# A four-layer decoder stack on one core: layer 2's first causal row maxima taken in half fills, with the second batch element's queries, keys and values made in between

## The chip, the cores and the metric

The kernel runs on one core of one Trainium2 chip. The metric is the device time of one execution in microseconds (us). Engines are called TensorE (PE in the profile, its weight loads PEld), VectorE (DVE), ScalarE (ACT) and GpSimd (POOL). PSUM has eight banks of 512 fp32 columns.

## The reference

Four transformer layers run one after the other on `x` of 2 batch elements x 512 tokens x 128 features. Only layer 2's causal self attention is touched, with the normalisation ahead of it (16 heads of 8 features):

```python
y = layer_norm(y + h, g3, be3)                # the end of layer 1
h = _ln(x, ln1_g, ln1_b)                      # layer 2
q = (h @ sa_wq + sa_bq).reshape(Bx, Lx, H, HD) * scale
k = (h @ sa_wk + sa_bk).reshape(Bx, Lx, H, HD)
v = (h @ sa_wv + sa_bv).reshape(Bx, Lx, H, HD)
q = _apply_rope(q, cos[:Lx], sin[:Lx])
k = _apply_rope(k, cos[:Lx], sin[:Lx])
a = _attn(q, k, v, causal=True).reshape(Bx, Lx, E)   # softmax needs each row's maximum
```

## The kernel before

Every engine has one instruction stream written out by hand; semaphores (`S(name)`) join them. A *half* is one batch element: 512 tokens in four tiles of 128 (`QB = 4`, `B = 2`). `x` holds tokens in partitions; `qT`, `kT` hold features in partitions.

**Making layer 2's queries and keys.** For each half in turn VectorE adds layer 1's last output to `x` (L1613), takes moments (`moments`, L1568 and L1571), normalises (`normal`, L1577) and multiplies by the gain (L1582); GpSimd adds the shift (`post_norm`, L479); then VectorE takes moments and normalises again for layer 2 (L1568 to L1577). GpSimd makes each reciprocal deviation (L473, L475). TensorE turns the half (`turn_half`, L619), ScalarE copies it to `xT` (L1317), TensorE projects queries and keys (L627, two passes per fp32 product, 512 columns each) and values (L635), ScalarE copies those out (L1506, L1326, L1510), and TensorE swaps the rotary pairs (L1217). GpSimd multiplies by cosines (`by_cosines`, L491); VectorE multiplies the swapped part by sines (L2000) and adds (L2002). GpSimd then makes four masked copies of a half's keys, `km` (`masked`, L496). In the VectorE stream both halves' normalisations stand ahead of the first rotation, and both rotations ahead of the first maximum.

**The maxima.** Heads are handled in 8 groups `g = 4*b + v` (batch element b, v of 4), four heads in each, one per band of 32 rows of the array. For a group, `causal_maxima` computes the scores of each block of 128 queries against its 128, 256, 384 or 512 keys in three fills, `FILLS = ((1, 0), (2,), (3,))`: four matmuls (L782), one per band, into four banks, and four full-height bf16 matmuls (L785) that add the causal mask to the diagonal. The eight banks are two sets of four, used in turn. For each block VectorE reduces the four banks to 128x4 negated maxima (L2012, `heads.max`), which frees the set. After the last group TensorE turns the maxima (`head_shifts`, L796), VectorE builds `q_shift` (L1696), and the exponentials begin (L826 scores, L1396).

TensorE waits for both halves' rotations before the first fill; so do ScalarE's masked keys `k1` (L1514), which the exponentials need. GpSimd adds value biases (L504) and the bias of the next addition (L487) after the masked keys.

Of the kernel before, what the change touches and what calls it, by code (L numbers as in the profile page):

```python
# [10 lines left out]
ALU = mybir.AluOpType  # L11
# [3 lines left out]
P = 128  # L15
D = 128
# [71 lines left out]
FILL_AT = {0: 2 * P, 1: 0, 2: 0, 3: 0}  # L88

ROUND_BEHIND, KEYS_BEHIND, VALUES_BEHIND = 3, 7, 8
# [50 lines left out]
def build(nc, ins, out, stop=99):  # L144
    ctx = ExitStack()
    with ctx:
        def sb(name, shape, dt=F32):
# [5 lines left out]

        families = {
            "one": (["L1.sa", "L1.ca"], dict(s=T, exp=T, t=T, pt=T, o=T, m=T, x=T)),
            "heads": (["L2.sa", "L2.ca"], dict(sc=0, max=4 * T, maxT=B * V, qs=B * V, s=8 * T, e=8 * T,
                                               pv=4 * T, o=B * V, ot=B * V, out=B * V)),
            "ints": (["L3.sa"], dict(s=PAIRS, nm=PAIRS, m=PAIRS, exp=2 * PAIRS, recip=PAIRS // 2, rounded=2 * PAIRS,
                                     pt=PAIRS, pv=PAIRS)),
# [260 lines left out]
        def _(pool):  # L420
# [72 lines left out]
            def masked(b):  # L493
                pool.wait_ge(S("L2.sa.rope"), 2 * b + 2)
                for v in range(V):
# [12 lines left out]
            if stop >= 1:  # L508
                for h in range(B):
                    rstds_of("L1.ln1", h)  # L510
                    post_norm("L1.ln1", 1, h)
                for h in range(B):
                    rstds_of("L1.ln2", h)
                    post_norm("L1.ln2", 3, h)
                    add_bias("L1.ff", "L1.ln2.x", h, h + 1)
                for h in range(B):
                    rstds_of("L1.ln3", h)
                    if h and stop >= 2:
                        pool.wait_ge(S("rope.loaded"), 32)
                        by_cosines(0, qT, 0)  # L520
                    post_norm("L1.ln3", 5, h)
                    if h and stop >= 2:
                        by_cosines(1, kT, 0)
                    if stop >= 2:
                        rstds_of("L2.ln1", h)
                if stop >= 2:
                    for side, src in enumerate((qT, kT)):
                        pool.wait_ge(S("L2.sa.rope"), side + 1)
                        by_cosines(side, src, 1)
                    masked(0)  # L530
                    masked(1)
                    value_biases()
                    for h in range(B):
                        add_bias("L2.ca0", "L2.ln1.xh", h, h + 1)
            def diagonals():

                for b in range(B):
# [76 lines left out]
        def _(pe):  # L614
# [143 lines left out]
            def project_half(name, wo, k, bank):  # L758
# [3 lines left out]
                    mm = pe.matmul(o, tile(xT, k * QB + t), wo, start=True, stop=True)  # L762
                mm.then_inc(S(f"{name}.o"), 1)

            def causal_maxima():

                for g in range(B * V):
                    b, v = divmod(g, V)
                    pe.wait_ge(S("L2.sa.keys"), g + 1)
                    for f, blocks in enumerate(FILLS):  # L770
                        bank = 4 * ((3 * g + f) % 2)
                        if f == 0 and g >= 1:
                            pe.wait_ge(S("heads.max"), QB * g - 1)
                        if f == 1 and g >= 1:
                            pe.wait_ge(S("heads.max"), QB * g)
                        if f == 2:
                            pe.wait_ge(S("heads.max"), QB * g + 2)
                        for qb in blocks:
                            c, n = FILL_AT[qb], (qb + 1) * P
                            for j in range(BANDS):  # L780
                                r = slice(BAND * j, BAND * (j + 1))
                                pe.matmul(ps[:, bank + j, c:c + n], qT[r, b * N + qb * P:b * N + (qb + 1) * P],  # L782
                                          km[r, v, b * N:b * N + n], start=True, stop=False)
                            for j in range(BANDS):
                                mm = pe.matmul(ps[:, bank + j, c + n - P:c + n], ident16[:, :], hide_q[:, :],  # L785
                                               start=False, stop=True)
                        mm.then_inc(S("L2.sa.fill"), 1)

            def head_shifts(name, quads, groups, bank):

# [418 lines left out]


            if stop >= 2:
                for k in range(B):
                    turn_half(xh, "L2.ln1.xh", k)
                    qkv("L2.sa", W["L2_xattn_sa_wq"], W["L2_xattn_sa_wk"], W["L2_xattn_sa_wv"], k)
                    for side, src in enumerate((qT, kT)):
                        pe.wait_ge(S("L2.sa.qk"), 2 * k + side + 1)
                        pe.matmul(ps[:, 2 * side + k, :], swap[:, :], half(src, k), start=True, stop=True  # L1217
                                  ).then_inc(S("L2.sa.swapped"), 1)
                pe.wait_ge(S("L2.sa.vraw"), B)
                pe.wait_ge(S("L2.sa.rope"), 2 * B)  # L1220
                causal_maxima()
                head_shifts("L2.sa", 4 * T - 1, range(V), lambda g: g)
                head_shifts("L2.sa", 4 * T, range(V, B * V), lambda g: g)
# [81 lines left out]
        def _(act):  # L1305
# [194 lines left out]
                state_out("L1.ff", col("L1_xattn_g2"), col("L1_xattn_be2"), [1])  # L1500
                hidden("L1.ff", ACT.Relu, "L1_xattn_b_ff1", HIDDEN_1, range(FC, B * FC))
            if stop >= 2:
                for k in range(B):
                    state_out("L2.sa", col("L2_xattn_ln1_g"), col("L2_xattn_ln1_b"), [k])
                    act.wait_ge(S("L2.sa.q.mm"), k + 1)
                    act.activation(half(qT, k), ps[:, 2 + k, :], ACT.Identity, scale=HEAD_SCALE, bias=bq_scaled[:, :]  # L1506
                                   ).then_inc(S("L2.sa.qk"), 1)
                    project_out(kT, "L2.sa.k.mm", 4, "L2.sa.qk", col("L2_xattn_sa_bk"), [k])
                    act.wait_ge(S("L2.sa.v.mm"), k + 1)
                    act.activation(v_one[:, :, k, :, 0:DH], ps[:, 6 + k, :].rearrange("p (t h d) -> p t h d", h=H, d=DH),  # L1510
                                   ACT.Copy).then_inc(S("L2.sa.vraw"), 1)
                act.wait_ge(S("L2.sa.rope"), 2 * B)
                for v in range(V):
# [42 lines left out]
        def _(dve):  # L1556
# [423 lines left out]
            if stop >= 1:  # L1980
                for k in range(B):
                    dve.wait_ge(S("L1.sa.v.mm"), k + 1)
                    dve.tensor_copy(half_rows(v_rows, k), bank_rows(6 + k)).then_inc(S("L1.sa.v"), 1)
                dve.wait_ge(S("spread.loaded"), 16)
                single_head()
                for k in range(B):
                    add_to_x("L1.ff", OUTPUTS_1, [k])
                    moments("L1.ln3", k, "L1.ff.x", 1)
                    normal("L1.ln3", k, to=4)
                    if stop >= 2:  # L1990
                        moments("L2.ln1", k, "L1.ln3.x", 1)
                        normal("L2.ln1", k)


            if stop >= 2:
                for k in range(B):
                    for side, src in enumerate((qT, kT)):
                        a, b = half(ta, side), half(tb, side)
                        dve.wait_ge(S("L2.sa.swapped"), 2 * k + side + 1)
                        then(dve.tensor_tensor(b, ps[:, 2 * side + k, :], sin_t[:, :], ALU.mult))  # L2000
                        dve.wait_ge(S("L2.sa.cos"), 2 * k + side + 1)
                        dve.tensor_tensor(half(src, k), a, b, ALU.add).then_inc(S("L2.sa.rope"), 1)  # L2002
                for g in range(B * V):
                    b, v = divmod(g, V)
                    for f, blocks in enumerate(FILLS):
                        bank = 4 * ((3 * g + f) % 2)
                        dve.wait_ge(S("L2.sa.fill"), len(FILLS) * g + f + 1)
                        for qb in blocks:
                            at = ((b * QB + qb) * V + v) * P
                            nm = neg_max[:, at:at + P].rearrange("p (j c) -> p j c", c=BAND)[:, :, spare_row(v)]  # L2010
                            c = FILL_AT[qb]
                            dve.tensor_reduce(nm, ps[:, bank:bank + 4, c:c + (qb + 1) * P], AX, ALU.max, negate=True  # L2012
                                              ).then_inc(S("heads.max"), 1)
# [172 lines left out]
```

## Time and profile before

| | us |
|---|---|
| median of 3 runs | 543.89 (541.73 to 545.26) |
| the profiled execution | 544.86 |
| its span, first to last instruction | 543.1 |
| busy: TensorE / VectorE | 398.2 / 365.9 |
| busy: ScalarE / GpSimd | 249.8 / 239.3 |

The span is from the first to the last instruction; the profiled execution took 1.8 us more than its span. An engine's busy time is a mean over stages with different limits: the stage of this change lies between 98 and 181 us of the span. What a group of instructions waited for stands in brackets behind it, as [idle before <-releaser].

### The profile page before, as it was taken

Reading aid. Unit: us, or ns where it says so; the run is one execution under the profiler, and the core shown is the slowest. Engines: PE = TensorE matmul, PEld = TensorE weight load, DVE = VectorE, ACT = ScalarE, POOL = GpSimd, SP = SyncE. Lnnn points to the kernel's source line nnn. Section 1 sums busy time; section 2 is a strip of 40 time slices with the busy share of each in tenths; the row PEclk is TensorE's granted clock in tenths of the full one; section 3 lists DMA queues with packets and bytes.
Section 4 is the critical chain, followed back from the end, with each engine's and each line's share of the span. In section 5 each row is a group of like instructions: output and inputs, shape, how many; then the busy total and the mean of one; then the engine's idle time right before and its main releaser. Section 6 shows DMA issues by size and latency. Waiting matters only on the chain.

```text
span 543.1 us, 8012 instructions
## 1 busy us (share of the span) xinstructions
PE 398.2 (73%) x2719; PEld 208.0 (38%) x2719; DVE 365.9 (67%) x810; ACT 249.8 (46%) x489; POOL 239.3 (44%) x377
## 2 busy tenths in 40 slices
PE   6979768847888999998988772566665664532697
PEld 3736644624334533434243550222232222221546
DVE  1654655364999711338584469999989898989542
ACT  2213423323100367660626327899977793334341
POOL 4033114355300244441301315999978895435420
PEclk9759855997899999999999995555555556665599
DMA  9400000000000000000000002798877586113301
GB/s 262 152 1 1 4 0 1 1 0 0 1 2 1 1 1 2 1 1 1 0 1 2 1 2 39 135 151 144 154 120 127 106 142 129 27 31 66 72 1 39
DMA packets 88975, 26.09 MB, mean 48 GB/s; under 512 B 81061, under 2 KB 88167, under 8 KB 88935
## 3 DMA queue, kind: packets, MB, share of 16 engines
q1 hardware_dynamic: 88935, 25.58, 24.1%
q8 instruction: 22, 0.36, 0.3%
q14 instruction: 18, 0.15, 0.1%
HBM read 5.61 MB, written 0.52 MB: 11 GB/s over the span
## 4 chain that ended last, share of the span: by engine, by line
PE 38%; DVE 32%; POOL 19%; issue 6%; ACT 2%; DMA 2%; POOLq 0%; DVEq 0%; ACTq 0%
POOL k_stack L565 13%; DVE k_stack L2012 8%; PE ps L826 5%; PE ps L841 4%; POOL stats L556 3%; PE ps L627 3%; PE ps L728 3%; DVE stats L2092 3%; PE ps L738 2%; DVE xh L1577 2%; DVE cr_max L1815 2%; DVE st L1568 2%; DVE cr_sum L1829 2%; PE ps L619 2%; PE ps L904 2%
## 5 line engine op out<-in xcount | busy, mean ns | idle before, releaser
L2092 DVE TENSOR_REDUCE stats<-ps 128x2 f32<-128x1024 f32 x64 | 77.7, 1213 | 2.4 <-PE ps L1255 2.0
L1533 ACT ACTIVATE e_buf<-ps,stats,sders 128x512 f32<-128x512 f32 x88 | 67.6, 773 | 18.4 <-POOL stats L556 18.4
L1275 PE MATMUL ps<-k_stack,q_stack 128*32 128x128 bf16 x512 | 38.2, 305 | 41.6 <-DVE k_stack L2105 41.4
L565 POOL TENSOR_SCALAR k_stack<-e_buf,stats 128x512 int16<-128x512 f32 x88 | 63.0, 728 | 2.1 <-DVE stats L2099 1.5
L1396 ACT ACTIVATE e_buf<-ps 128x1024 f32<-128x1024 f32 (+3 forms) x44 | 28.2, 710 | 58.5 <-PE ps L826 58.5
L1275 PEld LDWEIGHTS ps<-k_stack,q_stack 128*32 128x32 bf16 x512 | 22.1, 128 | 70.9 <-DVE k_stack L2105 68.8
L422 POOL TENSOR_SCALAR_AFFINE_SELECT e_buf<-e_buf 128x256 f32<-128x256 f32 x44 | 17.8, 413 | 67.2 <-ACT e_buf L1396 66.5
L473 POOL TENSOR_SCALAR rstd<-mv 128x4 f32<-128x4 f32 x18 | 4.1, 230 | 97.4 <-DVE mv L1571 94.4
L1255 PE MATMUL ps<-q_stack 32*128 32x512 bf16 x128 | 37.8, 591 | 12.2 <-ACT e_buf L1533 8.7
L2012 DVE TENSOR_REDUCE k_stack<-ps 128x4 f32<-128x1024 f32 (+3 forms) x32 | 45.0, 1481 | 2.5 <-PE ps L785 2.5
L782 PE MATMUL ps<-q_stack,qk 32*128 32x256 f32 (+3 forms) x256 | 27.6, 501 | 10.3 <-DVE k_stack L2012 7.4
L826 PE MATMUL ps<-k_stack,q_stack 32*128 32x512 f32 (+3 forms) x256 | 34.7, 478 | 0.6 <-ACT e_buf L1396 0.4
L1533 ACT ACTIVATE t_buf<-ps,stats,sders 128x512 f32<-128x512 f32 x40 | 30.8, 774 | 6.4 <-POOL stats L556 6.3
L556 POOL TENSOR_SCALAR stats<-stats,sders 128x2 f32<-128x2 f32 x64 | 23.7, 370 | 17.5 <-DVE stats L2092 17.4
L1703 DVE COPY v_rows<-ps 128x512 f32<-128x512 f32 x16 | 11.0, 689 | 29.8 <-PE ps L841 22.9
L1317 ACT ACTIVATE xT<-ps,cols 128x512 f32<-128x512 f32 x16 | 12.4, 776 | 38.5 <-PE ps L619 38.5
L1613 DVE TENSOR_TENSOR x<-ps,x 128x512 f32<-128x512 f32 x14 | 9.7, 690 | 30.3 <-PE ps L728 16.2
L627 PE MATMUL ps<-xT,wsq 128*128 128x512 f32 x36 | 25.7, 834 | 4.7 <-ACT xT L1317 4.7
L1577 DVE TENSOR_SCALAR xh<-x,mv,rstd 128x128 f32<-128x128 f32 x68 | 20.3, 361 | 12.8 <-POOL rstd L475 12.8
L565 POOL TENSOR_SCALAR k_stack<-t_buf,stats 128x512 int16<-128x512 f32 x40 | 28.3, 719 | 0.6 <-DVE stats L2099 0.2
L619 PE MATMUL ps<-ident,xh 128*128 128x128 f32 x80 | 15.6, 327 | 17.6 <-DVE xh L1577 16.5
L2105 DVE TENSOR_SCALAR k_stack<-k_stack 128x1024 bf16<-128x1024 int16 x64 | 27.9, 441 | 0.2
(269 smaller groups left out, 880.8 us busy)
## 6 DMA issues: line engine op xcount, KB each, us to landing
wsq<-in_squares SPq DMA_DIRECT2D x3, 384.0 KB, 5.0
k_stack<-k_stack SPq DMA_TRANSPOSE x64, 3.1
spread<-in_spread SPq DMA_DIRECT2D x1, 896.0 KB, 6.7
x<-in_x SPq DMA_DIRECT2D x1, 512.0 KB, 4.5
l_w<-in_L_xattn_W_ff SPq DMA_DIRECT2D x2, 256.0 KB, 7.1
l_w<-in_L_xattn_fc_w SPq DMA_DIRECT2D x2, 256.0 KB, 7.8
l_w<-in_L_xattn_ff_w SPq DMA_DIRECT2D x1, 512.0 KB, 8.8
out<-x SPq DMA_DIRECT2D x2, 256.0 KB, 2.3
```

Of the source, the lines that this page charges most:

```text
L556: pool.tensor_scalar(stats[:, 1, c:c + 2], stats[:, 0, c:c + 2], sders[:, 8:9], None, ALU.mult).then_inc(S("ints.m"), 1)
L565: pool.tensor_scalar(t_rows[n % TURNING][:, j, :], e_ring[n % len(e_ring)][:, j, :], stats[:, 2, c:c + 1], 0.0, ALU.mult, ALU.add).then_in ...
L627: return pe.matmul(ps[:, bank, :], w, half(xT, k), start=True, stop=True)
L826: mm = pe.matmul(ps[:, 2 * slot + j % 2, 0:N - kb * P], k1[r, v, b * N + kb * P:b * N + (kb + 1) * P], q_shift[r, b, v, kb * P:N], start=T ...
L1255: mm = pe.matmul(ps[:, 2 * (n % 3) + j % 2, :], tile(q_int, b * QB + qb)[r, :], k_band[r, v, b * N:(b + 1) * N], start=True, stop=True)
L1275: mm = pe.matmul(ps[BAND * band:BAND * (band + 1), 7, qb * P:(qb + 1) * P], v_band[:, kb, b, V * band + v, :], t_keys[n % len(t_keys)][:, ...
L1396: act.activation(e_ring[n % len(e_ring)][:, :, 0:N - kb * P], ps[:, 2 * (n % 3):2 * (n % 3) + 2, 0:N - kb * P], ACT.Exp).then_inc(S("heads ...
L1533: act.activation(e_ring[n % len(e_ring)][:, j, :], ps[:, 2 * (n % 3) + j, :], ACT.Exp, bias=stats[:, 1, c:c + 1], scale=sders[:, 8:9], acc ...
L1577: ins = dve.tensor_scalar(xh[:, t, :], x[:, t, :], mv[:, t, 0:1], rstd[:, t:t + 1], ALU.subtract, ALU.mult)
L2012: dve.tensor_reduce(nm, ps[:, bank:bank + 4, c:c + (qb + 1) * P], AX, ALU.max, negate=True).then_inc(S("heads.max"), 1)
L2092: dve.tensor_reduce(stats[:, 0, c:c + 2], ps[:, 2 * (n % 3):2 * (n % 3) + 2, :], AX, ALU.max, negate=True).then_inc(S("ints.nm"), 1)
L2105: dve.tensor_scalar(t_keys[n % len(t_keys)], t_turned[n % TURNING], QMAX, None, ALU.min).then_inc(S("ints.pt"), 1)
```

## The change

1. The first two of the eight groups (`HALVED = 2`) are taken in *half fills*: each fill of a group is made twice, for bands 0 and 1 and for bands 2 and 3, into two banks each. There are 12 half fills (`HALF_FILLS`), and they go round three pairs of banks, 0 to 5. A half fill may start once the third one before it has been reduced (`L2.sa.half`). VectorE's reductions of these are 128x2 out of two banks.
2. Banks 6 and 7 serve the second half meanwhile: TensorE turns it after half fill 2 (counted from 0), projects queries after 3 and keys after 5, swaps after 7 and 8, projects values after 9. VectorE normalises the second half after half fill 1 and rotates its queries after 7 and its keys after 9.
3. The other six groups are filled and reduced as before, through two sets of four banks.
4. VectorE applies gain and shift of layer 1's last normalisation itself (`scaled_and_shifted`), for both halves; GpSimd's `post_norm` of it is gone. The second half's gain, shift and layer 2 moments stand behind the first half's rotations in the VectorE stream.
5. GpSimd masks the first half's keys for groups 0 and 1, makes the second half's deviation, masks for groups 2 and 3, and then goes on to the second half's cosines and keys.

```diff
+HALVED = 2
+HALF_FILLS = [(g, blocks, pair) for g in range(HALVED) for blocks in FILLS for pair in range(2)]
+TURN_BEHIND, QUERIES_BEHIND, KEYS_MADE_BEHIND, SWAP_Q_BEHIND, SWAP_K_BEHIND, VALUES_MADE_BEHIND = 2, 3, 5, 7, 8, 9
+SECOND_NORMAL_BEHIND, ROPE_Q_BEHIND, ROPE_K_BEHIND = 1, 7, 9
...
+                by_cosines(0, qT, 0)
+                by_cosines(1, kT, 0)
+                masked(0, (0, 1))
+                rstds_of("L2.ln1", 1)
+                masked(0, (2, 3))
+                for side, src in enumerate((qT, kT)):
+                    pool.wait_ge(S("L2.sa.rope"), side + 1)
+                    by_cosines(side, src, 1)
+                masked(1)
+                value_biases()
...
+            def fill(g, blocks, bank, bands):
+                b, v = divmod(g, V)
+                for qb in blocks:
+                    c, n = FILL_AT[qb], (qb + 1) * P
+                    for i, j in enumerate(bands):
+                        r = slice(BAND * j, BAND * (j + 1))
+                        pe.matmul(ps[:, bank + i, c:c + n], qT[r, b * N + qb * P:b * N + (qb + 1) * P],
+                                  km[r, v, b * N:b * N + n], start=True, stop=False)
+                    for i, j in enumerate(bands):
+                        mm = pe.matmul(ps[:, bank + i, c + n - P:c + n], ident16[:, :], hide_q[:, :],
+                                       start=False, stop=True)
+                mm.then_inc(S("L2.sa.fill"), 1)
...
+                for n, (g, blocks, pair) in enumerate(HALF_FILLS):
+                    pe.wait_ge(S("L2.sa.keys"), g + 1)
+                    if n >= 3:
+                        pe.wait_ge(S("L2.sa.half"), n - 2)
+                    fill(g, blocks, 2 * (n % 3), (2 * pair, 2 * pair + 1))
+                    if n == TURN_BEHIND:
+                        turn_half(xh, "L2.ln1.xh", 1, bank=7)
+                    if n == QUERIES_BEHIND:
+                        pe.wait_ge(S("state.T"), state("L2.sa", 1))
+                        pe.wait_ge(S("L2.sa.vraw"), 1)
+                        project("L2.sa", W["L2_xattn_sa_wq"], 1, 6).then_inc(S("L2.sa.q.mm"), 1)
+                    if n == KEYS_MADE_BEHIND:
+                        project("L2.sa", W["L2_xattn_sa_wk"], 1, 7).then_inc(S("L2.sa.k.mm"), 1)
+                    if n == SWAP_Q_BEHIND:
+                        swapped(1, 0, 6)
+                    if n == SWAP_K_BEHIND:
+                        swapped(1, 1, 7)
+                    if n == VALUES_MADE_BEHIND:
+                        pe.wait_ge(S("L2.sa.rope"), 3)
+                        for t in range(QB):
+                            mm = pe.matmul(ps[:, 6, t * P:(t + 1) * P], tile(xT, QB + t), W["L2_xattn_sa_wv"],
+                                           start=True, stop=True)
...
+                def scaled_and_shifted(name, k, g):
+                    scale, shift = (spread[:, i, :].unsqueeze(1).broadcast_to([P, QB, D]) for i in (g, g + 1))
+                    dve.wait_ge(S(f"{name}.xh"), count(name, "xh") + k + 1)
+                    then(dve.tensor_tensor(half_rows(x, k), half_rows(xh, k), scale, ALU.mult))
+                    dve.tensor_tensor(half_rows(x, k), half_rows(x, k), shift, ALU.add).then_inc(S(f"{name}.x"), 1)
...
+                for side in range(2):
+                    rope(0, side, 2 * side)
+                scaled_and_shifted("L1.ln3", 1, 4)
+                moments("L2.ln1", 1, "L1.ln3.x", 1)
+                for n, (g, blocks, pair) in enumerate(HALF_FILLS):
+                    dve.wait_ge(S("L2.sa.fill"), n + 1)
+                    for ins in filled(g, blocks, 2 * (n % 3), slice(2 * pair, 2 * pair + 2)):
+                        last = ins
+                    last.then_inc(S("L2.sa.half"), 1)
+                    if n == SECOND_NORMAL_BEHIND:
+                        normal("L2.ln1", 1)
+                    if n == ROPE_Q_BEHIND:
+                        rope(1, 0, 6)
+                    if n == ROPE_K_BEHIND:
+                        rope(1, 1, 7)
```

## Rows read from the trace of the kernel before

**Rows 1.** Busy time by stretch: ahead of the maxima, and the maxima.
```profile
core 0: us, PE busy (x) PEld busy (x) DVE busy (x) ACT busy (x) POOL busy (x), PEclk, DMA share, GB/s
135.40:181.10 45.70, 37.86 (x378) 18.59 (x376) 45.03 (x33) 2.84 (x3) 5.74 (x6) 0.96 0.00 1
98.00:135.50 37.50, 24.89 (x130) 15.29 (x128) 19.20 (x60) 10.92 (x15) 17.58 (x21) 0.91 0.00 0
```

**Rows 2.** The chain that ended last, in order of time: start, us, what.
```profile
105.35 1.27 POOL x L479
...
133.67 0.71 PE ps L782 x8
...
139.65 41.43 DVE k_stack L2012 x29
```

**Rows 3.** VectorE's maxima by shape: count, busy us, mean ns, idle before.
```profile
L2012 DVE TENSOR_REDUCE k_stack<-ps 128x4 f32<-128x2048 f32 x8 | 18.2, 2281 | 0.2 <-PE ps L785 0.2
L2012 DVE TENSOR_REDUCE k_stack<-ps 128x4 f32<-128x1536 f32 x8 | 14.0, 1748 | 0.3 <-PE ps L785 0.3
L2012 DVE TENSOR_REDUCE k_stack<-ps 128x4 f32<-128x1024 f32 x8 | 9.7, 1215 | 1.9 <-PE ps L785 1.9
L2012 DVE TENSOR_REDUCE k_stack<-ps 128x4 f32<-128x512 f32 x8 | 5.4, 680 | 0.0
```

**Rows 4.** VectorE in order of time ahead of the maxima: start, us, instructions.
```profile
109.41 1.12 DVE L1577 TENSOR_SCALAR xh<-x,mv,rstd 128x128 f32<-128x128 f32 x4 [1.48 <-POOL rstd L475]
...
113.91 2.07 DVE L1577 TENSOR_SCALAR xh<-x,mv,rstd 128x128 f32<-128x128 f32 x4 [1.46 <-POOL rstd L475]
...
121.88 0.68 DVE L2000 TENSOR_TENSOR tb<-ps,sin_t 128x512 f32<-128x512 f32 x1
...
135.52 1.83 DVE L2012 TENSOR_REDUCE k_stack<-ps 128x4 f32<-128x1024 f32 x2 [1.95 <-PE ps L785]
```

**Rows 5.** GpSimd in order of time in the same stretch.
```profile
114.10 1.29 POOL L491 TENSOR_TENSOR ta<-qk,cos_t 128x512 f32<-128x512 f32 x1 [0.23 <-ACT qk L1506]
...
119.77 1.04 POOL L475 TENSOR_TENSOR rstd<-rstd,minus_half 128x4 f32<-128x4 f32 x1
...
129.90 3.14 POOL L496 TENSOR_SCALAR q_stack<-qk,band_mask 128x512 f32<-128x512 f32 x4
```

**Rows 6.** TensorE in order of time: parts of one group's fills, at steady pace.
```profile
151.07 0.71 PE L782 MATMUL ps<-q_stack,qk 32*128 32x256 f32 x8 [0.29 <-DVE k_stack L2012]
...
151.72 0.40 PE L785 MATMUL ps<-hide_q,ident 128*128 128x128 bf16 x4
...
152.05 0.50 PE L782 MATMUL ps<-q_stack,qk 32*128 32x128 f32 x8
...
152.48 0.40 PE L785 MATMUL ps<-hide_q,ident 128*128 128x128 bf16 x4
...
154.91 1.14 PE L782 MATMUL ps<-q_stack,qk 32*128 32x512 f32 x8 [0.47 <-DVE k_stack L2012]
...
155.98 0.40 PE L785 MATMUL ps<-hide_q,ident 128*128 128x128 bf16 x4
```

**Rows 7.** TensorE later, in layer 2's cross attention: two bands alone.
```profile
260.08 1.08 PE L904 MATMUL ps<-k_stack,k 32*77 32x512 f32 x4 [0.66 <-DVE k_stack L1696]
```

**Rows 8.** TensorE in order of time around the first half's swaps.
```profile
113.93 1.05 PE L635 MATMUL ps<-wsq,xT 128*128 128x128 f32 x8
114.82 1.88 PE L1217 MATMUL ps<-qk,swap 128*128 128x512 f32 x4
122.02 1.11 PE L619 MATMUL ps<-ident,xh 128*128 128x128 f32 x4 [5.32 <-DVE xh L1577]
```

**Rows 9.** Busy time by short stretch, with TensorE's granted clock (PEclk).
```profile
118.30:121.70 3.40, 0.00 (x0) 0.00 (x0) 1.89 (x12) 0.00 (x0) 2.24 (x3) 1.00 0.00 0
121.70:125.10 3.40, 2.21 (x6) 1.30 (x7) 2.85 (x6) 0.78 (x1) 0.00 (x0) 0.51 0.00 0
...
131.90:135.40 3.50, 1.73 (x24) 1.11 (x24) 1.64 (x2) 1.79 (x2) 2.87 (x5) 1.00 0.00 0
135.40:138.80 3.40, 3.40 (x22) 1.37 (x20) 2.98 (x3) 2.84 (x3) 3.40 (x5) 0.50 0.02 5
```

More of the change, by code:

```diff
@@ L515, in _ @@
                     add_bias("L1.ff", "L1.ln2.x", h, h + 1)
-                for h in range(B):
[L517 to L534, printed above, removed]
+                rstds_of("L1.ln3", 0)
+                rstds_of("L2.ln1", 0)
+                rstds_of("L1.ln3", 1)
+                pool.wait_ge(S("rope.loaded"), 32)
+                by_cosines(0, qT, 0)
[8 more added lines that the diff above has]
+                value_biases()
+                for h in range(B):
+                    add_bias("L2.ca0", "L2.ln1.xh", h, h + 1)
             def diagonals():
@@ L765, in causal_maxima @@
             def causal_maxima():
-                for g in range(B * V):
-                    b, v = divmod(g, V)
+                for g in range(HALVED, B * V):
+                    done = QB * (g - HALVED)
                     pe.wait_ge(S("L2.sa.keys"), g + 1)
                     for f, blocks in enumerate(FILLS):
[L771 to L775, printed above, removed]
-                        if f == 2:
[L777 to L787, printed above, removed]
@@ L789, in head_shifts @@
+                        if f == 2:
+                            pe.wait_ge(S("heads.max"), done + 2)
+                        fill(g, blocks, bank, range(BANDS))
             def head_shifts(name, quads, groups, bank):
@@ L1985, in _ @@
                 single_head()
[L1986 to L1992, printed above, removed]
-            if stop >= 2:
[L1996 to L2003, printed above, removed]
-                    b, v = divmod(g, V)
-                    for f, blocks in enumerate(FILLS):
[L2006 to L2013, printed above, removed]
@@ new lines, in _, with rope, filled @@
+                moments("L1.ln3", 0, "L1.ff.x", 1)
+                normal("L1.ln3", 0)
+                scaled_and_shifted("L1.ln3", 0, 4)
+                moments("L2.ln1", 0, "L1.ln3.x", 1)
+                normal("L2.ln1", 0)
+                add_to_x("L1.ff", OUTPUTS_1, [1])
+                moments("L1.ln3", 1, "L1.ff.x", 1)
+                normal("L1.ln3", 1)
+            if stop >= 2:
+                def rope(k, side, bank):
+                    a, b, dst = half(ta, side), half(tb, side), half((qT, kT)[side], k)
+                    dve.wait_ge(S("L2.sa.swapped"), 2 * k + side + 1)
+                    then(dve.tensor_tensor(b, ps[:, bank, :], sin_t[:, :], ALU.mult))
+                    dve.wait_ge(S("L2.sa.cos"), 2 * k + side + 1)
+                    dve.tensor_tensor(dst, a, b, ALU.add).then_inc(S("L2.sa.rope"), 1)
+                def filled(g, blocks, bank, bands):
+                    b, v = divmod(g, V)
+                    for qb in blocks:
+                        at = ((b * QB + qb) * V + v) * P
+                        nm = neg_max[:, at:at + P].rearrange("p (j c) -> p j c", c=BAND)[:, bands, spare_row(v)]
+                        c, n = FILL_AT[qb], bands.stop - bands.start
+                        ins = dve.tensor_reduce(nm, ps[:, bank:bank + n, c:c + (qb + 1) * P], AX, ALU.max, negate=True)
+                        yield ins
+                for side in range(2):
+                    rope(0, side, 2 * side)
[12 more added lines that the diff above has]
+                        rope(1, 1, 7)
+                for g in range(HALVED, B * V):
+                    for f, blocks in enumerate(FILLS):
+                        m = 3 * (g - HALVED) + f
+                        dve.wait_ge(S("L2.sa.fill"), len(HALF_FILLS) + m + 1)
+                        for ins in filled(g, blocks, 4 * (m % 2), slice(0, BANDS)):
+                            ins.then_inc(S("heads.max"), 1)
```

54 lines of the change are left out of this document (35 added, 19 removed).

## The prediction

> **What bounds the kernel now.** I read the busy time by stretch first. From 135.4 to 181.1 us VectorE is busy 45.0 of 45.7 us, while TensorE is busy 37.9 [rows 1]: the maxima are VectorE's. From 98 to 135.5 VectorE is busy only 19.2 of 37.5 us [rows 1]. The chain of work then shows how these two join: one chain leads through additions, norms, projections and rotations to the first fill at 133.67, and from 139.65 it is 29 reductions without a break, 41.43 us, to 181.08 [rows 2]. The first reduction starts at 135.52 [rows 4]. So the stage ends when VectorE has done 45 us of maxima after a start that waits for both batch elements, although the first element's keys are ready some ten microseconds sooner. What the change can give is read at 181.08, the end of the last reduction: everything behind it (turned maxima, exponentials, the later layers) starts from there and keeps its order.
>
> **The change, part by part.** I follow the new order and carry one clock, the time in the span.
>
> *The shift on VectorE.* GpSimd's shift takes 1.27 us [rows 2]; on VectorE it is a 128x512 operation like the sine product, 0.68 [rows 4]. With the hop it saves 0.62 for the first half, and everything up to the second half's layer 1 norm moves forward by 0.62: that norm starts at 113.91 - 0.62 = 113.29. It still meets the first cosine product on GpSimd, so it keeps its 2.07 us and ends at 115.36.
>
> *The first rotation earlier.* The second half's gain, shift, moments and layer 2 norm no longer stand ahead of the rotation. Its inputs are there: the swaps start at 114.82 - 0.62 = 114.20 [rows 8], the two cosines end by 116.1 (two of 1.29 [rows 5] from 113.5). Four operations of 0.68 with their hops, 2.75 us, end at 118.13. Two masked copies follow on GpSimd; one costs 0.65 to 0.8 (3.14 for four [rows 5]).
>
> *A collision.* VectorE's gain and shift now run beside GpSimd's masked copies. The row shows that such work blocks: the same four normalising operations took 2.07 us where a GpSimd product started 0.19 us into them, and 1.12 where none did [rows 4, 5]. I price it at 0.6 (about one masked copy) here, and again at 0.6 where the second layer 2 norm meets the masks for groups 2 and 3; the bounds for each are 0, if the two miss each other, and 1.3, two masked copies. The reductions I leave alone: beside GpSimd's copies the first two took 1.83 [rows 4], their unhindered length by [rows 3].
>
> By the Trainium skill (SBUF — State Buffer, Who interferes with whom), whichever starts first holds the shared ports for its whole instruction when VectorE has two SBUF inputs or a two-port mode. By that rule gain and shift could each meet a copy, 1.3 instead of 0.6, and the last reduction would come 0.7 later; the trace's 2.07 against 1.12 is a blocking of about one instruction.
>
> So the first half fill starts at 119.6, and VectorE ends gain, shift (2.0 with the collision) and moments (1.3) at 121.5.
>
> *Half fills on TensorE.* A fill of 256 columns takes 0.65 from its start to its masks, of 128 0.43, of 512 1.07; 384 lies between, 0.86 [rows 6]. The four masks occupy 0.33 [rows 6], two of them 0.22. Does a matmul group on two bands cost half of one on four? The trace has two bands alone: 512 columns, 1.08 us [rows 7], beside 1.14 for four [rows 6]. So it costs the same, and a group's maxima cost TensorE nearly twice. Half fills occupy 0.65 + 0.22 + 0.43 + 0.22 = 1.52, 0.86 + 0.22 = 1.08 and 1.07 + 0.22 = 1.29; four of each are 15.5 us, where two whole groups took 1.74 + 1.19 + 1.40 = 4.3 each, 8.7 together.
>
> *The second half's work on TensorE.* Turning 0.44 (four passes of 0.11), two projections and two swaps of 0.86 each (1.88 for two swaps with the tail of the last [rows 8]), values 0.87 (eight passes within 1.05 [rows 8]): 4.7 us. With the half fills that is 20.3 us from 119.6. By the new order there is one wait in it: behind half fill 2 (done at 123.7) TensorE needs the second half's norm. The moments are there at 121.5, GpSimd's deviation (0.23 and 1.04 [rows 5]) at 122.9; VectorE reduces half fills 0 and 1 first, then norms for 1.1 + 0.6 and ends at 125.3. TensorE loses 1.7 us there, and the half fills 3 to 11 stand behind that turn. ScalarE's copies lie under half fill 3 and later ones.
>
> *Half reductions on VectorE.* From [rows 3], 512 elements more cost 0.533 us, so 1.04 ns each and 0.146 fixed; back to back, 29 of them fit in 41.43 us, 0.08 less each than their durations. So a half reduction of 256, 512, 768, 1024 elements takes 0.33, 0.60, 0.86, 1.13: 11.7 us for the twelve half fills against 11.2 for two whole groups, 0.5 us for eight more instructions. The 256 is below every row, by the line through the others; were it as dear as the 512, it would add 0.27 four times.
>
> *Who sets the pace there.* VectorE has 11.7 + 1.7 + 2 x 1.4 = 16.2 us from 121.5; TensorE has 20.3 + 1.7 from 119.6. TensorE sets it: half fill 11 starts at 140.3 and is reduced by 142.8. The first whole fill needs the bank pairs of half fills 9 and 10; it starts near 141.8, takes 1.8, and VectorE waits 0.8 us and starts on it at 143.6. Six groups follow at 5.6 us each (5.92 by [rows 3] less four overlaps of 0.08): the last reduction ends at 177.4. The second half's keys, masks, values and ScalarE's four `k1` copies lie under these 34 us.
>
> *The clock.* TensorE was granted full speed until 121.7 and half of it (1.2 GHz) after a gap of 5.3 us without a matmul [rows 8, 9]; it fell again at 135.4 after a stretch in which it was busy 1.73 of 3.5 us [rows 9]. Over the maxima it was at 0.96 on average [rows 1], so that fall was short. In the new order TensorE idles from about 116.1 to 119.6, 3.5 us, between those two cases. I take one fall, 121.7 to 125.1, at a cost of 0.95: the half fills in it take double, part of it under the wait for the norm. The bounds are none (0) and a fall from 118.3 to 128.6 (3.1).
>
> **Sum.** 177.4 + 0.95 = 178.4 against 181.08: 2.7 us sooner. The profiled execution took 544.86, so 542.2; the median of the runs is 0.97 below that execution, so 541.2.
>
> **The rivals.**
>
> *Nothing is won.* The clock is at half from 118.3 to 128.6, or both collisions cost 1.3 (1.4 more) and the 256-element reductions 1.1: the last reduction ends near 180.7, and the time is 543.5. For it: two falls in this very stretch [rows 9]. Against: the new gap is shorter than the one that cost two steps. Chance 0.18.
>
> *More is won.* Full speed throughout gives 177.4, or 540.2, and cheap collisions up to 1.5 more, 538.7. Chance 0.14.
>
> *VectorE-bound after all.* If the second pair's matmuls overlapped the masks of the first, so that a half fill cost about half a fill, VectorE would run through: 121.5 + 16.2 + 0.8 + 33.7 = 172.2, 8.9 us sooner, 535.0. What speaks against it is that a mask is 128 rows high and starts only when the bands have finished [rows 6]. The Trainium skill, TensorEngine Tiling (Array Packing), Key Properties, says that a change of tiling mode drains the array. By that rule this way is closed, and the trace agrees: 1.07 us from a 512-column start to its masks. Chance 0.11.
>
> *Slower.* TensorE, at two bands and waiting for VectorE, is held at half speed through all half fills (118.3 to 143): they and the second half's work take twice as long, the last reduction ends at 187.8, and the time is 550.6. It costs more than it gives from the point where the half clock lasts beyond 129.5. For it: a stretch busy for half its time lost the clock [rows 9]. Against: from 119.6 on TensorE is nearly always busy, and in the maxima it kept 0.96 of full speed on average with 37.9 busy of 45.7 us [rows 1]. Chance 0.09.
>
> **How the numbers follow.** My forecast has the remaining 0.48. A change of 1% is 5.4 us, about what a measurement of this kernel can tell from none. Faster by over 1% is the VectorE-bound way and a thread of the second rival, 0.12; slower by over 1% 0.09; within 1% 0.79. The forecast's own range is 539.5 to 543. The range for the time leaves out the VectorE-bound way and the slower one: 537.8 at the cheap end of the collisions, 546.3 for a clock at half until about 134.
>
> **What would show it.** In the profile after: GpSimd's L479 work at 105 and 117 gone; first half fill at 119.6 and first half reduction at 121.5 (was 135.52); half fills of 1.3 us for 512 columns; TensorE waiting 1 to 2 us for the norm behind half fill 2; VectorE idle some 5 us in all between 121.5 and 143.6; whole groups at 5.6 us as before; last reduction near 178. The prediction is wrong if a half fill costs much less than 1.3 us, if the granted clock stays at half beyond 128, or if the time after the last reduction (363.8 us to the end of this execution) is not the same.

## The result

| | us |
|---|---|
| median after (4 runs) | 557.16 (554.87 to 557.68) |
| median before, measured with it (4 runs) | 543.88 (541.73 to 545.26) |
| ratio after / before | 1.027, 95% interval 1.023 to 1.032 |
| profiled execution after | 554.87, its span 553.1 |

The change made the kernel 2.7% slower. The stage itself can be compared from one event to another: from the first half's last layer 1 norm (L1577 before, L1621 after) to the end of the last maximum. Before it runs from 103.43 to 181.08, 77.6 us. After it runs from 99.18 to 190.80, 91.6 us: 14.0 us more, where the prediction had 2.7 less. What follows is the same to half a microsecond (362.0 us of span before, 362.3 after). So the profiled spans differ by 10.0 us only: the stage began 4.25 us sooner in this one execution, because the clock had come back sooner in the code ahead of it, which the change does not touch (in all thirteen traces of this document the norm starts about 9 to 10.5 us after that return, wherever it falls). The busy time of the same window (us, the engines, granted clock, DMA share, GB/s), of the kernel before:

```profile
89.80:94.40 4.60, 4.60 (x7) 1.92 (x6) 2.79 (x13) 1.57 (x3) 1.45 (x3) 0.50 0.00 0
```

and of the kernel after, where the clock was already back at full:

```profile
89.80:94.40 4.60, 3.73 (x26) 2.77 (x25) 0.43 (x1) 1.37 (x2) 2.53 (x2) 1.00 0.01 4
```

The busy time by stretch of the kernel after, to be read beside [rows 1, 9]: the pause, the start of the first half fill, the rest of the half fills, the whole fills up to the clock's return, and the rest.

```profile
core 0: us, PE busy (x) PEld busy (x) DVE busy (x) ACT busy (x) POOL busy (x), PEclk, DMA share, GB/s
112.00:116.00 4.00, 0.00 (x0) 0.00 (x0) 3.90 (x7) 0.00 (x0) 1.17 (x2) 1.00 0.00 0
116.00:117.20 1.20, 1.17 (x10) 0.74 (x10) 1.17 (x5) 0.00 (x0) 0.98 (x1) 0.98 0.00 0
117.20:152.70 35.50, 35.27 (x111) 13.54 (x108) 15.72 (x28) 6.72 (x8) 9.15 (x12) 0.50 0.00 1
152.70:161.50 8.80, 8.80 (x57) 3.95 (x56) 5.82 (x5) 0.57 (x1) 3.46 (x3) 0.50 0.01 2
161.50:190.80 29.30, 24.04 (x252) 12.30 (x248) 29.30 (x22) 0.00 (x0) 0.00 (x0) 1.00 0.00 1
```

TensorE was busy for 35.27 of 35.5 us and was granted half its clock (1.2 GHz) all the while. It got the other half back at 161.5, 8.8 us after the whole fills had begun. VectorE had work for 15.7 of those 35.5 us, so it was not what TensorE waited for.

VectorE in order of time answers to [rows 4]. The bracket behind a reduction is the time it stood idle for a fill:

```profile
109.03 3.04 DVE L1621 TENSOR_SCALAR xh<-x,mv,rstd 128x128 f32<-128x128 f32 x4 [1.48 <-POOL rstd L481]
...
117.83 1.02 DVE L2062 TENSOR_REDUCE k_stack<-ps 128x2 f32<-128x512 f32 x2
...
129.67 1.23 DVE L2062 TENSOR_REDUCE k_stack<-ps 128x2 f32<-128x1024 f32 x1 [3.19 <-PE ps L778]
...
136.35 1.02 DVE L2062 TENSOR_REDUCE k_stack<-ps 128x2 f32<-128x512 f32 x2 [3.12 <-PE ps L778]
...
160.48 30.31 DVE L2062 TENSOR_REDUCE k_stack<-ps 128x4 f32<-128x2048 f32 x21 [0.80 <-PE ps L778]
```

The first reduction stands 18.65 us after the norm (before: 32.09), so the early start was had. TensorE in order of time, answering to [rows 6]: the start of the first half fill at full clock, the second half's turning, and two half fills at half clock.

```profile
116.03 0.70 PE L775 MATMUL ps<-q_stack,qk 32*128 32x256 f32 x4 [4.21 <-POOL q_stack L502]
...
122.46 1.11 PE L623 MATMUL ps<-ident,xh 128*128 128x128 f32 x4 [0.23 <-DVE xh L1621]
...
127.23 2.08 PE L775 MATMUL ps<-q_stack,qk 32*128 32x512 f32 x4
129.24 0.39 PE L778 MATMUL ps<-hide_q,ident 128*128 128x128 bf16 x2
129.56 2.08 PE L775 MATMUL ps<-q_stack,qk 32*128 32x512 f32 x4
```

A half fill of 512 columns is 2.33 us from start to start, against 1.29 forecast at full clock. The chain of work runs through TensorE alone from 122.5 to 160.5.

### The profile page after: what moved, and what is told of

Its sections match the earlier page's. It is cut to its first block, busy times and chain, and to the rows that moved or that the text cites. A ratio compares the mean times of both kernels' runs of the same rounds, so it can differ in the third digit from the quotient of the medians.

```text
span 553.1 us, 8030 instructions
## 1 busy us (share of the span) xinstructions
PE 413.1 (75%) x2719; PEld 210.4 (38%) x2719; DVE 369.6 (67%) x820; ACT 249.5 (45%) x489; POOL 237.0 (43%) x375
## 4 chain that ended last, share of the span: by engine, by line
PE 42%; DVE 29%; POOL 18%; issue 6%; ACT 2%; DMA 2%; POOLq 0%; DVEq 0%; ACTq 0%
POOL k_stack L569 13%; DVE k_stack L2062 6%; PE ps L873 5%; PE ps L775 5%; PE ps L888 4%; POOL stats L560 3%; PE ps L631 3%; PE ps L732 3%; DVE stats L2164 3%; PE ps L742 2%; DVE xh L1621 2%; DVE cr_max L1859 2%; PE ps L623 2%; DVE cr_sum L1873 2%; PE ps L766 2%
## 5 line engine op out<-in xcount | busy, mean ns | idle before, releaser
L2164 DVE TENSOR_REDUCE stats<-ps 128x2 f32<-128x1024 f32 x64 | 77.6, 1213 | 2.4 <-PE ps L1299 2.0
L1577 ACT ACTIVATE e_buf<-ps,stats,sders 128x512 f32<-128x512 f32 x88 | 67.6, 774 | 19.1 <-POOL stats L560 19.1
L1319 PE MATMUL ps<-k_stack,q_stack 128*32 128x128 bf16 x512 | 37.9, 305 | 42.6 <-DVE k_stack L2177 42.6
L2062 DVE TENSOR_REDUCE k_stack<-ps 128x4 f32<-128x1024 f32 (+7 forms) x40 | 46.7, 1219 | 21.9 <-PE ps L778 21.8
L775 PE MATMUL ps<-q_stack,qk 32*128 32x256 f32 (+3 forms) x256 | 45.0, 608 | 9.1 <-DVE k_stack L2062 4.8
L1577 ACT ACTIVATE t_buf<-ps,stats,sders 128x512 f32<-128x512 f32 x40 | 30.8, 773 | 6.4 <-POOL stats L560 6.3
L1621 DVE TENSOR_SCALAR xh<-x,mv,rstd 128x128 f32<-128x128 f32 x68 | 21.2, 375 | 11.5 <-POOL rstd L481 11.5
```

What stands on the lines that cost most here:

```text
L775: pe.matmul(ps[:, bank + i, c:c + n], qT[r, b * N + qb * P:b * N + (qb + 1) * P], km[r, v, b * N:b * N + n], start=True, stop=False)
L1319: mm = pe.matmul(ps[BAND * band:BAND * (band + 1), 7, qb * P:(qb + 1) * P], v_band[:, kb, b, V * band + v, :], t_keys[n % len(t_keys)][:, ...
L1577: act.activation(e_ring[n % len(e_ring)][:, j, :], ps[:, 2 * (n % 3) + j, :], ACT.Exp, bias=stats[:, 1, c:c + 1], scale=sders[:, 8:9], acc ...
L1621: ins = dve.tensor_scalar(xh[:, t, :], x[:, t, :], mv[:, t, 0:1], rstd[:, t:t + 1], ALU.subtract, ALU.mult)
L2062: ins = dve.tensor_reduce(nm, ps[:, bank:bank + n, c:c + (qb + 1) * P], AX, ALU.max, negate=True)
L2164: dve.tensor_reduce(stats[:, 0, c:c + 2], ps[:, 2 * (n % 3):2 * (n % 3) + 2, :], AX, ALU.max, negate=True).then_inc(S("ints.nm"), 1)
```

## The experiments

Two theories stood against each other. **W (width)**: matmuls on two of the four bands leave TensorE at half clock however busy it is. **G (gap)**: the clock was lost to the 4.2 us pause ahead of the half fills, and would have held without it.

**The pause filled** (`gap_filled`).

```diff
                 pe.wait_ge(S("L2.sa.vraw"), 1)
+                for _ in range(4):
+                    pe.matmul(ps[:, 1, :], ident[:, :], half(xT, 0), start=True, stop=True)
                 first_maxima_of_self()
```

> The changed kernel with four extra full-height matmuls of 512 columns (results unused, into a free bank) in TensorE's pause between the first half's swaps and the first half fill. Theory W (width): TensorE loses its full clock because the half fills run on two of four bands; the clock falls within them all the same, and the time stays at 555 to 557 us. Theory G (gap): the pause of 4 us takes the clock away; with it filled the clock stays at full speed through the half fills, the stage goes as predicted, and the time is near 540 us.

Measured: 555.94 us, ratio to before 1.024 (1.018 to 1.030), within W's 555 to 557. TensorE in order of time:

```profile
110.34 3.77 PE L1265 MATMUL ps<-xT,ident 128*128 128x512 f32 x8
114.48 0.71 PE L775 MATMUL ps<-q_stack,qk 32*128 32x256 f32 x4 [0.38 <-POOL q_stack L502]
115.13 0.28 PE L778 MATMUL ps<-hide_q,ident 128*128 128x128 bf16 x2
115.34 0.49 PE L775 MATMUL ps<-q_stack,qk 32*128 32x128 f32 x4
115.76 0.28 PE L778 MATMUL ps<-hide_q,ident 128*128 128x128 bf16 x2
115.98 0.71 PE L775 MATMUL ps<-q_stack,qk 32*128 32x256 f32 x4
```

and the busy time and the clock by stretch (this execution's records list full speed as 0.95):

```profile
110.00:114.80 4.80, 4.42 (x12) 1.74 (x12) 4.70 (x8) 0.00 (x0) 1.70 (x3) 0.95 0.00 0
114.80:117.80 3.00, 3.00 (x26) 1.65 (x24) 2.54 (x12) 0.00 (x0) 2.07 (x4) 0.95 0.00 0
117.80:150.00 32.20, 31.23 (x92) 11.62 (x88) 14.26 (x21) 6.50 (x8) 7.59 (x9) 0.50 0.00 1
```

With 0.4 us of pause left and TensorE busy all of 114.8 to 117.8, the clock fell at 117.8 all the same, two half fills in, and stayed down until 155.3. So G does not account for the loss: without the pause the time is that of the changed kernel. That a pause can take the clock as well is not excluded by this; `both_pairs` below bears on it.

**Half fills alone** (`halves_alone`): the kernel before, with groups 0 and 1 in half fills (`first_maxima_of_self`, banks 0 to 5) and nothing between them; `causal_maxima` keeps groups 2 to 7.

```diff
+                first_maxima_of_self()
                 causal_maxima()
```

> halves_waiting without the extra waits: the half fills of groups 0 and 1 alone, in the order of the kernel before. Theory W: the clock stays at half through them; 2 us less than halves_waiting for the waits, 557 to 558 us, some 3 per cent slower than before; the changed kernel minus this is then what the new order alone gives back (about -1 to -3 us).

Measured: 558.17 us against 542.08, ratio 1.027 (1.021 to 1.032), 0.2 above the range expected. The half fills run from 129.3 to 155.3; the stretch at half clock, which ends 6.2 us behind them:

```profile
130.80:161.50 30.70, 30.70 (x129) 11.93 (x128) 15.61 (x19) 3.06 (x3) 5.93 (x6) 0.50 0.00 1
```

In the old order the half fills alone cost the whole loss. The stage took 93.6 us; in the changed kernel, with the new order, it took 91.6, so the new order gave 2.0 us back.

**The same with the idle bands at work** (`halves_waiting` against `halves_four_bands`). Both wait for the end of the half fill before (the extra matmuls of successive half fills share banks 6 and 7). The second, to which the last four added lines belong, also runs each block on the other two bands, results unused:

```diff
                 for n, (g, blocks, pair) in enumerate(HALF_FILLS):
...
+                    if n >= 1:
+                        pe.wait_ge(S("L2.sa.fill"), n)
...
+                    for i, j in enumerate(j for j in range(BANDS) if j not in bands):
+                        r = slice(BAND * j, BAND * (j + 1))
+                        pe.matmul(ps[:, 6 + i, c:c + n], qT[r, b * N + qb * P:b * N + (qb + 1) * P],
+                                  km[r, v, b * N:b * N + n], start=True, stop=True)
```

> The kernel before, in its old order, with groups 0 and 1 taken in half fills and nothing put between them; each half fill also waits for the end of the one before it (so that it compares with halves_four_bands). W: the clock stays at half from about 135 us until some 9 us after the last half fill; two groups take 27 us on TensorE where VectorE needs 11.7, and the time is 560 to 564 us. If width does not matter, the clock comes back after one step of 3.4 us as in the kernel before; two groups take 17, and the time is 549 to 551 us.

> halves_waiting with the two idle bands given the same matmuls into banks 6 and 7, results unused: the same order and waits, the same fills, all four bands at work, and by the rows of before no time added at equal clock. W: the clock comes back within one or two steps, and the time is 549 to 552 us. If width does not matter it equals halves_waiting within 1 us, or is slower.

Measured: 559.63 us (ratio 1.032, 1.027 to 1.036) and 551.54 us (1.016, 1.009 to 1.023). The first of these is just below the 560 to 564 expected, the second within its 549 to 552. The stretches of the half fills, of `halves_waiting`:

```profile
132.10:159.80 27.70, 26.20 (x92) 9.65 (x92) 12.32 (x16) 2.85 (x3) 6.15 (x7) 0.50 0.00 1
```

and of `halves_four_bands`, where the clock came back at 140.5, after 6.8 us (the last 1.6 us of the second line are whole fills):

```profile
133.70:140.50 6.80, 6.50 (x40) 2.64 (x40) 2.90 (x5) 2.84 (x3) 5.73 (x6) 0.50 0.01 2
140.50:154.20 13.70, 12.51 (x125) 5.51 (x124) 9.83 (x11) 0.00 (x0) 0.00 (x0) 1.00 0.01 2
```

The share of time in which TensorE is busy is nearly the same in the first line (26.2 of 27.7, 95%) and in the last two (19.0 of 20.5, 93%). Both kernels lost the clock within 2 us of their first half fill, behind a pause of 2.5 to 2.9 us. With two bands it stayed at half from 132.1 to 162.8, 30.7 us, and came back 4.0 us after four bands had started; with four bands it stayed at half for 6.8 us. Twice the work within the same instructions' time made the kernel 8 us faster. So W is shown for what it says of the time at half clock: what kept the clock down is that half of the bands stood empty. Whether the rows count or the number of running matmuls, this pair cannot tell, since both double. The trace of the kernel before speaks for the rows: there full-height matmuls that run one behind the other (L738, from 88.84 on, in the window of that kernel shown with the result) had the full clock back at 94.4, 5.6 us later, so one matmul at a time is enough where it fills them.

**Both pairs issued together** (`both_pairs`): the changed kernel, with the matmuls of a block on all four bands before its masks; banks and reductions still go by pairs.

```diff
+                    for k, qb in enumerate(FILLS[f]):
...
+                        for pair in range(2):
+                            if k == 0 and 2 * w + pair >= 3:
+                                pe.wait_ge(S("L2.sa.half"), 2 * w + pair - 2)
+                            for i in range(2):
+                                j = 2 * pair + i
+                                r = slice(BAND * j, BAND * (j + 1))
+                                pe.matmul(ps[:, banks[pair] + i, c:c + n], qT[r, b * N + qb * P:b * N + (qb + 1) * P],
+                                          km[r, v, b * N:b * N + n], start=True, stop=False)
+                        for pair in range(2):
+                            for i in range(2):
+                                mm = pe.matmul(ps[:, banks[pair] + i, c + n - P:c + n], ident16[:, :], hide_q[:, :],
+                                               start=False, stop=True)
```

> The changed kernel with the matmuls of both pairs of bands issued together (four bands at work at once), through the same three pairs of banks, each pair still reduced by itself; TensorE turns the second half after whole fill 1, projects queries and keys after 2, swaps after 3 and 4, values after 4. W: the clock, lost in the pause, comes back within one or two steps; a group costs TensorE 4.3 us instead of 7.8, VectorE waits some 3 us in all; the last reduction is 5 to 7 us sooner than in the kernel before relative to layer 1's last norm, and the time is 537 to 540 us. G: the pause still takes the clock, and it stays away as long as in the changed kernel, some 44 us: 552 us or more.

Measured: 540.45 us, ratio 0.997 (0.993 to 1.000). The changed kernel's ratio is 1.027, so it is 3% faster than that one, and G's 552 us or more is out. Against the kernel before it is 1.3 us, which can hardly be told from none, and just outside the 537 to 540 expected. The stage took 75.8 us, 1.9 less than before, where 5 to 7 less were expected: the clock was at half from 118.7 to 129.0, across the first fills, longer than forecast, and again from 139.2 to 146.1:

```profile
115.00:129.00 14.00, 11.10 (x55) 5.53 (x56) 11.58 (x25) 0.95 (x2) 4.78 (x6) 0.63 0.01 1
129.00:139.20 10.20, 8.38 (x66) 3.93 (x65) 7.82 (x13) 3.17 (x5) 3.79 (x4) 1.00 0.00 1
139.20:146.10 6.90, 6.90 (x44) 2.90 (x44) 4.46 (x4) 3.27 (x3) 6.17 (x7) 0.51 0.00 0
```

The first fall came 0.8 us into the first fill, behind an unfilled pause of 4.2 us, with all four bands at work. So here a pause did cost the clock, and in the changed kernel it may have taken it first as well. What the half fills added is that it was lost without the pause too (`gap_filled`), and that it did not come back for 44.4 us.

**Its pauses filled** (`both_pairs_gap`, `both_pairs_warm`, `both_pairs_warmer`): full-height matmuls, results unused, put where TensorE waits. The first has four in the pause ahead of the first fill, the second one more ahead of the first fill of group 2, the third one more behind whole fill 1 (in this order in the diff).

```diff
+                for _ in range(4):
+                    pe.matmul(ps[:, 1, :], ident[:, :], half(xT, 0), start=True, stop=True)
                 first_maxima_of_self()
...
+                    if w == 5:
+                        pe.wait_ge(S("L2.sa.rope"), 4)
+                        pe.matmul(ps[:, 7, :], ident[:, :], half(xT, 0), start=True, stop=True)
...
                     if w == 1:
+                        pe.matmul(ps[:, 6, :], ident[:, :], half(xT, 0), start=True, stop=True)
                         turn_half(xh, "L2.ln1.xh", 1, bank=7)
```

> both_pairs with four extra full-height matmuls of 512 columns (results unused) in TensorE's pause between the first half's swaps and the first fill. In both_pairs the clock was at half from 118.7 to 129.0 us, where TensorE was busy nearly all the time, and again from 139.2 to 146.1. If the pause causes the first fall, and four bands at work keep the clock, it is at full speed there; by the fills' rows that is worth 2 to 3 us of both_pairs' time, so 537 to 538.5 us where both_pairs has 540.5. If the first fills lose the clock even so (as in gap_filled), the time is both_pairs' within 1 us.

> both_pairs_gap with one more unused full-height matmul while TensorE waits for the last paired reductions, ahead of the first fill in the old manner, where the clock fell the second time. If that wait of 1.7 us causes the second fall, it goes too, worth another 1 to 1.5 us: 536 to 537.5 us. Otherwise the time is that of both_pairs_gap.

> both_pairs_warm once more, with more rounds: 1.3 per cent faster than the kernel before, 0.9 to 1.7.

> both_pairs_warm with one more unused matmul while TensorE waits 1.2 us for the second half's norm behind whole fill 1, where the clock of both_pairs_gap fell at 122.7 us and that of both_pairs_warm did not. If that wait is what takes the clock in some of the executions, the slow ones among them go: the median is 1 to 2 us below both_pairs_warm. If not, the two are equal within 1 us.

| | median us | before beside it | ratio (95%) | stage, us |
|---|---|---|---|---|
| `both_pairs_gap` | 538.86 | 542.08 | 0.990 (0.982 to 0.998) | 75.7 |
| `both_pairs_warm` | 536.24 | 542.08 | 0.987 (0.980 to 0.994) | 70.9 |
| `both_pairs_warm_again` | 536.93 | 542.24 | 0.992 (0.988 to 0.995) | 70.9 |
| `both_pairs_warmer` | 535.82 | 542.24 | 0.988 (0.982 to 0.995) | 70.9 |

Filling the first pause alone did not keep the clock in the profiled execution (half from 122.7 to 129.6 and from 139.8 to 146.6), and its time against `both_pairs` on another set of runs settles nothing. With the wait ahead of group 2 filled too, the clock stayed full through the stage in the three profiled executions. The fall at 122.7 is not explained by that filling, which comes later: `both_pairs_warm` has the same code and the same wait of 1.18 us there, and kept its clock. The turning behind that wait, of `both_pairs_gap` and then of `both_pairs_warm`:

```profile
123.41 1.11 PE L623 MATMUL ps<-ident,xh 128*128 128x128 f32 x4 [1.18 <-DVE xh L1637]
...
119.80 0.66 PE L623 MATMUL ps<-ident,xh 128*128 128x128 f32 x4 [1.18 <-DVE xh L1640]
```

So what a wait of this length does to the clock differs from one execution to another, and how often each kernel keeps it is not known from three traces. The repetition came to 0.8% where 0.9 to 1.7 was expected. The added matmul of `both_pairs_warmer` cannot be told from none. The best is 6.4 us faster than the kernel before; its stretch, up to group 2 and from there:

```profile
109.00:134.00 25.00, 23.28 (x141) 11.10 (x139) 22.99 (x41) 4.79 (x8) 10.42 (x12) 1.00 0.00 1
134.00:170.00 36.00, 29.57 (x306) 14.84 (x304) 35.14 (x27) 3.95 (x4) 6.82 (x8) 1.00 0.01 1
```

**How much of that is the clock** (`before_warm`): the kernel before with its own two pauses filled.

```diff
                 for k in range(B):
+                    for _ in range(5 * k):
+                        pe.matmul(ps[:, 1, :], ident[:, :], half(xT, 0), start=True, stop=True)
                     turn_half(xh, "L2.ln1.xh", k)
...
                 pe.wait_ge(S("L2.sa.vraw"), B)
+                for _ in range(3):
+                    pe.matmul(ps[:, 7, :], ident[:, :], half(xT, 0), start=True, stop=True)
                 pe.wait_ge(S("L2.sa.rope"), 2 * B)
```

> The kernel before with unused full-height matmuls in two pauses of TensorE: five between the first half's swaps and the second half's turning, three between the second half's swaps and the first fill. It tells how much of both_pairs_warm's gain is the clock and how much the order. In the kernel before the clock was at half for 6.8 and 3.4 us there; by the rows of that stretch (projections 3.78 us at half against 1.98, turning 1.11 against 0.66, first fills 0.5 to 1 us late) the clock is worth 2.5 to 3 us: 539 to 540 us where the kernel before has 542. If it is 536 or less, the order in both_pairs_warm gives nothing.

Measured: 539.00 us, ratio 0.994 (0.991 to 0.997), the stage 73.9 us, at full clock throughout. So of the stage's 6.8 us (77.65 to 70.87) the clock is 3.8, and the order with four bands at work, the shift on VectorE included, 3.0. This split is read from profiled executions, one of `before_warm` and three of the others, which took 70.9 each; the intervals of the whole times, 0.991 to 0.997 here and 0.988 to 0.995 for `both_pairs_warm_again`, overlap. The interleaving is worth something in the stage; the half fills were not.

**The shift alone** (`shift_alone`).

```diff
-                    normal("L1.ln3", k, to=4)
+                    normal("L1.ln3", k)
+                    scaled_and_shifted("L1.ln3", k, 4)
...
-                    post_norm("L1.ln3", 5, h)
```

> The kernel before with only one part of the change: VectorE applies the gain and the shift of layer 1's last norm, for both halves; GpSimd's shift is gone; the order is the old one. By the prediction's step it saves 0.6 us for each half on the chain, 1.2 in all: 0.1 to 0.4 per cent faster than the kernel before. If GpSimd's cosine product then blocks VectorE's two-input operations, it saves nothing.

Measured: 542.63 us against 542.08, ratio 0.998 (0.995 to 1.002): nothing that can be told. The stage took 77.3 us, 0.3 less where 1.2 was forecast. With the shift gone from GpSimd, both cosine products follow one another there, and VectorE's norm meets the two, which costs 1.0 us more than meeting one:

```profile
111.12 3.04 DVE L1576 TENSOR_SCALAR xh<-x,mv,rstd 128x128 f32<-128x128 f32 x4 [1.47 <-POOL rstd L475]
...
111.30 2.52 POOL L491 TENSOR_TENSOR ta<-qk,cos_t 128x512 f32<-128x512 f32 x2 [0.22 <-ACT qk L1505]
```

## Why the prediction was wrong

*The step that failed* is the one on the clock. It asked only how long TensorE would pause, took one fall of 3.4 us at 0.95 us (the fall of the kernel before at 121.7 had itself lasted until 128.5), and let the half fills count as full activity because TensorE would be busy nearly all the time. The clock was at half for 44.4 us, 117.15 to 161.53. At 116.0, after the pause, the first half fill still ran at full speed (0.70 for 256 columns), and `gap_filled` showed that the clock is lost without the pause too. The argument against the slower rival, full clock through the maxima with 37.9 of 45.7 us busy [rows 1], came from fills on four bands and was carried over to two. The two-band matmuls at full clock of [rows 7] were 1.08 us between full-height work, a turning at 258.77 and a projection at 261.10.

The Trainium skill (TensorE: Matmul & The Clock Gate, Part 1, What's actually happening) says that the gate is set by how busy the PE has been recently. The rows differ if busy means the share of time: 35.27 of 35.5 us at 0.50 here. The measurement decides: how much of the array is filled counts too.

*The rival that came true* is the slower one, chance 0.09, and only in part. Two bands at work and half speed through all half fills is what happened; that TensorE would be "waiting for VectorE" is not, for it was busy 35.27 of 35.5 us. Its size was too small, 550.6 against 557.2, mostly by its own sum: it says that the half fills and the second half's work take twice as long, but it adds 10.4 us, about half of the stretch from 118.3 to 143 as it would be at full clock. From the first half fill to the first whole one the forecast had 22.2 us (119.6 to 141.8), and the trace has 36.7 (116.03 to 152.69), 14.5 more. Besides, the clock came back 8.8 us after the last half fill, not with it, and three whole fills ran at half speed too.

*The terms, from norm to last reduction* (forecast 75.0 us with its clock term, measured 91.6):

- The start. The first half fill came 16.85 us after the norm, forecast 16.2: 0.7 late. The collision of the second layer 1 norm with both cosine products (3.04 instead of 2.07) costs 1.0; the rotation and the first masked copy came 0.3 closer behind it than forecast. The two collisions with the masks, priced at 0.6 each, are not on this path: the first cost 0.37 (the shift, 1.06 instead of 0.69), the second nothing (the layer 2 norm took 1.11).
- The twelve half fills and the second half's work, from the first half fill to the first reduction of group 2: 39.8 us (116.03 to 155.79), forecast 24.95 (119.6 to 143.6, and 0.95 for the clock): 14.8 more. At full clock the term looks right: `gap_filled` shows 0.65 + 0.21 + 0.42 + 0.22 = 1.50 for the first half fill, forecast 1.52. Two bands do cost what four cost: 0.65 from the start of the 256 columns to their masks in both cases.
- Within that term, the wait for the second half's norm behind half fill 2, forecast 1.7, was 0.23, since TensorE itself came late.
- The six whole groups: 35.0 us (155.79 to 190.80), forecast 33.8: 1.2 more, at the half clock.
- The half reductions were right: 0.69 for 512 elements and 0.42 for 256, both within 0.02 of the line through [rows 3].

0.7 + 14.8 + 1.2 is the whole difference of 16.7. The 14.8 and the 1.2 are the clock's: the step that could be compared at full clock fits (1.50 against 1.52), and at half clock a half fill of 512 columns is 1.8 times its forecast. That everything behind the stage would keep its time was right.

## What to carry to other kernels

A band left empty is not only lost throughput: on this chip it kept TensorE at half clock while it was busy without a pause. When a PSUM shortage suggests fills in halves, split the buffers and the reductions but issue the matmuls so that all bands run together, as `both_pairs` does. That alone does not hold the clock: there it fell behind a pause with four bands at work too. An empty pause of TensorE ahead of a stage that it sets can be worth filling with unused full-height matmuls: that alone gave the old kernel 0.6%.

## What the runs showed of the hardware

- The clock was lost with TensorE busy 3.0 of 3.0 us on half fills (`gap_filled`, 114.8 to 117.8); in the changed kernel it stayed at half over 35.5 us with 99% busy. It came back 4.0 to 8.8 us after four bands were at work again (`halves_waiting` 4.0, `gap_filled` 5.1, `halves_alone` 6.2, the changed kernel 8.8).
- With the second pair of bands given unused work in the same instruction slots, it came back after 6.8 us, in the midst of the half fills (`halves_four_bands`); without it, the clock was at half for 30.7 us (`halves_waiting`).
- The same wait of 1.18 us ahead of the second half's turning was accompanied by a fall to half clock in one execution and not in another (`both_pairs_gap`, `both_pairs_warm`).
- VectorE's norm of four 128x128 tiles took 1.11 us alone, 2.07 beside one 1.29 us GpSimd product and 3.04 beside two (2.52): beside products the four operations take about three quarters of the products' time longer, so moving work off GpSimd can put its other work in VectorE's way.
